# A new order for the first look-ups, transposes and grams, and a second ScalarE pass that writes the rounded tables to PSUM

## What is computed

```
e = stack([tbl_f[ids[:, f]] for f in range(27)], axis=1)      # 2048 x 27 x 128
z = e @ e^T of each sample, the entries below the diagonal    # 2048 x 351
h = concat([z, dense_ctx], axis=1)                            # 2048 x 367
h = relu(h @ W_top1 + b_top1); h = relu(h @ W_top2 + b_top2)  # 512, then 256 wide
y = h @ W_top3
```

## Time and profile before

| | |
|---|---|
| Median of 3 runs | 360.65 us (360.56 to 360.74) |
| Profiled execution, its own time | 360.54 us |
| Its span, first to last instruction | 358.7 us |
| PE busy with matmuls | 333.7 us, 93% |
| POOL busy | 250.4 us, 70% |
| DVE busy | 246.3 us, 69% |
| ACT busy | 144.4 us, 40% |

### The profile page before, as it was taken

One profiled execution on the slowest core, in us unless ns is written; L12 is line 12 of the kernel. 1 busy time (PEld: TensorE's weight loads), 2 busy tenths in 40 slices (PEclk: granted clock), 3 DMA queues, 4 the chain that ended last, 5 costly groups with the idle time before them and its releaser, 6 DMA issues.

```text
span 358.7 us, 13616 instructions
## 1 busy us (share of the span) xinstructions
PE 333.7 (93%) x6094; PEld 303.4 (85%) x6094; DVE 246.3 (69%) x329; ACT 144.4 (40%) x265; POOL 250.4 (70%) x271
## 2 busy tenths in 40 slices
PE   1879699989999989999999999999999999999896
PEld 0779499978999979898889989999899989997775
DVE  3959979975488935878197965968387955961142
ACT  2536524444433433335343453435343353435320
POOL 5777777777777777777777777777777777777200
PEclk9969989999999999999999999999999999999999
DMA  6997744534333353443333452434533443322100
GB/s 184 306 318 196 205 136 107 102 93 91 83 93 82 90 99 75 96 96 80 93 88 82 115 85 77 105 84 81 102 89 83 99 98 74 84 55 55 27 3 1
DMA packets 26155, 36.86 MB, mean 103 GB/s; under 512 B 8451, under 2 KB 20099, under 8 KB 26098
## 3 DMA queue, kind: packets, MB, share of 16 engines
q0 software_dynamic: 8448, 17.32, 20.5%
q1 hardware_dynamic: 17506, 18.16, 20.1%
q10 hardware_dynamic: 144, 0.52, 0.4%
HBM read 35.97 MB, written 0.01 MB: 100 GB/s over the span
## 4 chain that ended last, share of the span: by engine, by line
PE 57%; POOL 26%; issue 10%; DVE 3%; DMA 3%; ACT 1%; DVEq 0%; ACTq 0%
POOL rows L450 26%; PE e_banks L482 25%; PE w_banks L543 9%; PE g_banks L513 8%; PE w_banks L554 7%; PE e_banks L494 6%; DMA rows<-in_tbl,idx 2%; DVE one_hot L672 2%; PE w_banks L532 1%; DVE zt L686 1%; DMA idx<-in_idx 1%; ACT et L340 0%; ACT h L333 0%; ACT et L350 0%; DVE a L720 0%
## 5 line engine op out<-in xcount | busy, mean ns | idle before, releaser
L450 POOL DMA_INDIRECT rows<-in_tbl,idx x264 | 249.6, 945 | 82.9 <-issue 78.0
L672 DVE TENSOR_TENSOR one_hot<-ids_wide,row_no 128x1024 fp32r<-128x1024 int32 x160 | 186.3, 1215 | 76.5 <-PE e_banks L482 72.5
L482 PE MATMUL e_banks<-one_hot,table_hi 128*128 128x256 f32 x672 | 172.2, 294 | 3.4 <-issue 3.4
L482 PE MATMUL e_banks<-one_hot,table_lo 128*128 128x256 f32 x672 | 167.0, 287 | 0.0
L482 PEld LDWEIGHTS e_banks<-one_hot,table_hi 128*128 128x128 f32 x672 | 131.4, 196 | 4.4 <-issue 4.2
L482 PEld LDWEIGHTS e_banks<-one_hot,table_lo 128*128 128x128 f32 x672 | 131.6, 196 | 0.2
L350 ACT ACTIVATE et<-e_banks 128x256 f32<-128x256 f32 x84 | 57.9, 689 | 89.3 <-PE e_banks L482 89.3
L340 ACT ACTIVATE et<-e_banks 128x512 f32<-128x512 f32 (+1 forms) x68 | 45.0, 664 | 52.3 <-PE e_banks L494 51.5
L513 PEld LDWEIGHTS g_banks<-et 128*26 128x26 f32 x4096 | 41.7, 103 | 17.7 <-issue 13.3
L513 PE MATMUL g_banks<-et 128*26 128x26 f32 x4096 | 50.0, 191 | 1.8 <-DVE zt L686 1.3
L494 PE MATMUL e_banks<-ident,rows 128*128 128x128 f32 x264 | 43.0, 285 | 5.5 <-DMA rows<-in_tbl,idx 5.5
(11 more groups left out here) (25 smaller groups left out, 67.7 us busy)
## 6 DMA issues: line engine op xcount, KB each, us to landing
ids_wide<-in_ids SPq DMA_DIRECT2D x80, 128.0 KB
et<-in_kept_tables SPq DMA_DIRECT2D x10, 512.0 KB, 10.1
rows<-in_tbl,idx POOLq DMA_INDIRECT x264
et<-in_kept_tables ACTq DMA_DIRECT2D x1, 512.0 KB, 3.9
a1T<-in_ids SPq DMA_DIRECT2D x4, 128.0 KB, 10.8
w<-in_w SPq DMA_DIRECT2D x2, 256.0 KB
w<-in_W_top SPq DMA_DIRECT2D x1, 512.0 KB
w<-in_w SPq DMA_DIRECT2D x1, 222.0 KB
```

Source lines behind the costliest of these rows:

```text
L450: pool.indirect_dma_start(rows[:, k % RING, a, :], None, tables[f], bass.IndirectOffsetOnAxis(ap=idx[:, t, f:f + 1], axis=0)).then_inc(row ...
L482: last = nc.tensor.matmul(e_bank[n % E_BANKS][:, 0:UNIT], part[:, q, c, :], one_hot[:, hot_slot(o, piece), c % PIECE, :], start=(c == 0 an ...
L672: nc.vector.tensor_tensor(one_hot[:, hot_slot(o, piece), :, :], ids_place(o).unsqueeze(1).broadcast_to([P, PIECE, UNIT]), row_no[:, piece ...
```

## The change

1. **The order of the start.** Two look-ups stand ahead of the first transposes as before; the next six come at (n - 1) * 2 // 3 for look-up n, one or two behind each transposed chunk, in place of 1 + (n - 2) * 7 // 10. The eight gram pieces of tile 0 are laid over two ticks from tick 5 in place of four ticks from tick 6. The look-ups of unit 1 are spread anew by the same planner; from `("T", 2, 0)` on the list is the same as before.
2. **The rounded tables.** The steps `("HI", n)` and `ident_r` are gone. Right behind each rounding, ACT copies `table_hi` to the PSUM banks itself, one instruction of 1024 columns. Table 10, the last, now goes to `w_banks` like table 9, and ACT waits there for the rest of table 9. The zeroing of `g_banks` is gone; the first grams wait for `lo_ready` 9 in its place, that is, for the last rest that reads `g_banks`.
3. **POOL's lead.** Chunk k now waits for chunk k - ahead, with ahead = min(7, 3 + k // 4): chunks 3 to 6 wait too, and up to chunk 15 the lead is shorter.

```diff
 RING = 7
+LEAD_AT_FIRST = 3
...
-    FIRST = [("HI", n) for n in range(AHEAD)]
+    FIRST = []
     for n, q in enumerate(looked_up(0)):
-        at = 1 + (n - AHEAD) * 7 // 10
-        step = [("OH", 0, q)] + [("HI", n + AHEAD)]
-        if n == FIRST_LOOK_UPS - 1:
-            step += [("HI", m) for m in range(n + AHEAD + 1, NOH)]
         if n < AHEAD:
-            FIRST += step
+            FIRST.append(("OH", 0, q))
         else:
-            look_ups[at].append(step)
+            look_ups[(n - 1) * 2 // 3].append([("OH", 0, q)])
     for t in range(LAST_TILE):
-        at = TILE_AT[t + 1] + (t == 0)
+        at = TILE_AT[t + 1]
+        ticks = 2 if t == 0 else 4
...
-            grams[at + p * 4 // G_PIECES].append(step)
+            grams[at + p * ticks // G_PIECES].append(step)
...
-        hi_banks = [g_banks, w_banks]
+        hi_banks = [w_banks if n == NOH - 1 else (g_banks, w_banks)[n % 2] for n in range(NOH)]
+        LAST_IN_G = max(n for n in range(NOH) if hi_banks[n] is g_banks)
...
-                if k >= RING:
-                    pool.wait_ge(t_filled, k - RING + 1)
+                ahead = min(RING, LEAD_AT_FIRST + k // 4)
+                if k >= ahead:
+                    pool.wait_ge(t_filled, k - ahead + 1)
...
                 if t == 0 and p == 0:
-                    pe.wait_ge(g_banks_zeroed, 1)
+                    pe.wait_ge(lo_ready, LAST_IN_G + 1)
...
-            def rounded_table(n):
-                pe.wait_ge(hi_ready, n + 1)
...
-                    last = nc.tensor.matmul(hi_banks[n % 2][:, i, :], ident_r[:], upper[:, i * BANK:(i + 1) * BANK],
-                                            start=True, stop=True)
-                last.then_inc(hi_copied, 1)
...
             def keep_upper(n):
                 act.wait_ge(table_in[n], 16)
                 nc.scalar.activation(table_hi[:, TABLE_ORDER[n], :, :], stage(n), ACT.Copy).then_inc(hi_ready, 1)
+                act.wait_ge(hi_ready, n + 1)
+                if n == NOH - 1:
+                    act.wait_ge(lo_ready, n)
+                elif n >= 2:
+                    act.wait_ge(lo_ready, n - 1)
+                nc.scalar.activation(hi_banks[n][:, :, :].rearrange("p k d -> p (k d)"),
+                                     table_hi[:, TABLE_ORDER[n], :, :].rearrange("p c d -> p (c d)").bitcast(F32),
+                                     ACT.Copy).then_inc(hi_copied, 1)
```

More of the change, by code:

```diff
@@ L235, in dlrm_tower @@
         ident = sb("ident", [P, P])
-        ident_r = sb("ident_r", [P, P], F32R)
         row_no_i = sb("row_no_i", [P, OC], I32)
@@ L293, in dlrm_tower @@
         ids_aside_in = {o: sem(f"ids_aside_in{o}") for o in range(IDS_RING, FIRST_LOOK_UPS)}
-        g_banks_zeroed = sem("g_banks_zeroed")
         table_in = [sem(f"table_in{q}") for q in range(NOH)]
@@ L297, in dlrm_tower @@
         hi_copied = sem("hi_copied")
-        ident_r_ready = sem("ident_r_ready")
         lo_ready = sem("lo_ready")
@@ L556, in layer2 @@
                 last.then_inc(w_filled, 1)
-            def rounded_table(n):
-                pe.wait_ge(hi_ready, n + 1)
[L560 to L564, removed]
-                    last = nc.tensor.matmul(hi_banks[n % 2][:, i, :], ident_r[:], upper[:, i * BANK:(i + 1) * BANK],
-                                            start=True, stop=True)
-                last.then_inc(hi_copied, 1)
             pe.wait_ge(ident_ready, 1)
-            pe.wait_ge(ident_r_ready, 1)
             for s in STEPS:
-                if s[0] == "HI":
-                    rounded_table(s[1])
                 if s[0] == "T":
@@ L656, in keep_rest @@
                                         stage(n).rearrange("p c d -> p (c d)"),
-                                        hi_banks[n % 2][:, :, :].rearrange("p k d -> p (k d)"),
+                                        hi_banks[n][:, :, :].rearrange("p k d -> p (k d)"),
                                         ALU.subtract).then_inc(lo_ready, 1)
-                if n == NOH - 1:
-                    dve.wait_ge(lo_ready, NOH)
-                    nc.vector.memset(g_banks[:], 0.0).then_inc(g_banks_zeroed, 1)
             def make_one_hot(o):
@@ L728, in _ @@
             nc.vector.tensor_copy(row_no[:], row_no_i[:]).then_inc(row_no_ready, 1)
-            dve.wait_ge(ident_ready, 1)
-            nc.vector.tensor_copy(ident_r[:], ident[:]).then_inc(ident_r_ready, 1)
             dve.wait_ge(row_no_ready, 1)
```

## The result

The changed kernel takes **363.46 us** in the median (360.44 to 364.37, 19 runs), the kernel before 360.21 us in the same comparison (359.51 to 361.94, 19 runs): ratio **1.0063**, 95% interval 1.0048 to 1.0079. The prediction said 360.6. The times fall into two groups: nine runs at 360.4 to 362.6 and ten at 363.4 to 364.4. No run of the kernel before lies in the upper group, and the profiled execution (363.64 us, span 361.8) does.

A forecast was written before the change was run, and what follows sets the result against it. POOL's gather pace was taken as the bound before chunk 24, PE and POOL nearly together behind it. POOL 0, start 0, from chunk 14 on 0 left 360.5 us; the median 0.1 above gave 360.6, range 360.1 to 361.5.

The forecast's parts named there:

- The list is the same from chunk 10 on, so the rest is the same.: From chunk 10 on: PE, some 5 us ahead, waits for POOL's rows, reaches chunk 14 as before, and nothing later changes.
- from chunk 14 on 0: Term of the sum for everything from chunk 14 to the end: no change, 0 us.
- my rivals: The clock falls (0.14 briefly, 0.07 longer), POOL held (0.04), ACT late (0.03), chunk 24's landing in time (0.10).
- The lead holds nothing: POOL's gathers at the start: the shorter lead delays none, 1.9 us to spare at chunk 0's transposes; term 0.
- PE's early lead turns into waiting: Chunks 10 to 14: PE's 5 us of lead becomes waiting for POOL's rows, gaining nothing.
- ScalarE's pass, taken as 1.06: ACT's table copy at the start: 1.06 us each, between 0.56 and 1.9.
- The start: Start of the program: chunk 7 transposed at 47.0 instead of 51.66, chunk 10 at about 60 instead of 64.89; term 0.
- Chunk 14: PE's wait for rows at chunk 14: 2 to 3 us, ending at 79.53 as before.
- that rival: After chunk 14's longer wait PE's clock falls: briefly 361.0 us, chance 0.14; at length or twice 362.5, chance 0.07.
- The landing of chunk 24: Rival: if chunk 24's rows land in time, PE runs 1.1 us earlier to the last chunk: 360.2 us, chance 0.10.
- two bounds within 0.7 to 1.0 us of each other: Behind chunk 24, PE's work and POOL's gathers bound the kernel almost equally; an earlier PE could get 0.4 us.

The follow-up runs named there:

- f3: Kernel before with only ScalarE's second pass in place of the table products, old order and lead, TensorE's stream 53 instructions shorter: 364.00 us, ratio 1.0102.
- f4: Kernel before with 203 instructions of already met waits added on TensorE, spread over the transposes: 374.25 us, ratio 1.0370.
- e12: Kernel before with only POOL's new, shorter lead of the gathers: 360.42 us, ratio 0.9990.
- g1: Kernel before with only the new order of look-ups, transposes and grams, stream length unchanged: 360.65 us, ratio 0.9998.
- f1: The changed kernel itself, run again without edits: 361.43 us, ratio 1.0048 to the kernel before.
- f2: Changed kernel with 53 instructions (106 already met waits) put back at TensorE's start: 361.60 us, ratio 1.0033 to the kernel before.
- e11: Kernel before with only ScalarE's second pass, plus 53 instructions of met waits given back to TensorE: 361.60 us, ratio 1.0017.
- e4: Kernel before with only ScalarE's second pass, old order and lead, TensorE's stream 53 instructions shorter: ratio 1.0058.
- e6, e2: Kernel before with 203 instructions of already met waits on TensorE, ahead of transposes and at the start: ratio 1.0275.
- e9: The changed kernel itself, run again as base for its padded forms: ratio 1.0086 to the kernel before.

## Why the prediction was wrong

**The step that failed** is "The list is the same from chunk 10 on, so the rest is the same." The list of work is; the position of its instructions in the stream is not. What was said to be free is the removal of 53 instructions 300 us earlier, and with them went the cover of a block's load. In the prediction's sum this is the term "from chunk 14 on 0": it was 3.1 us of the span, of which 0.44 had come about by the last transposes and 2.5 are the stands. They are shown for the profiled run. That they lift half of the runs by 2 to 3 us rests on the counts and on f3 and f4. None of my rivals had it, and the page had the queue in its section 3. A piece of 0.31 us of plain issue stood in the last stretch of the kernel before, where there is no other work. I had no reason for it and did not ask.

**Right.** The lead holds nothing (e12, and no piece over 0.30 us in POOL's line). PE's early lead turns into waiting; the order alone is worth nothing (g1, within 0.2%). ScalarE's pass, taken as 1.06:

```profile
L586 ACT ACTIVATE w_banks<-table_hi x6: 1027/1028/1030, 10.2 to 42.6; 128x1024 f32<-128x1024 f32 x6
L586 ACT ACTIVATE g_banks<-table_hi x5: 1027/1028/1029, 6.5 to 34.7; 128x1024 f32<-128x1024 f32 x5
```

**Mis-sized.** *The start.* Chunk 7 at 47.0 came at 50.87, chunk 10 at 60 came at 63.62. The rows are DVE's, ACT's and PE's timelines:

```profile
28.29 1.22 DVE L664 TENSOR_TENSOR one_hot<-a1T,row_no 128x1024 fp32r<-128x1024 int32 x1 [1.87 <-PE e_banks L481]
```

```profile
42.55 1.03 ACT L586 ACTIVATE w_banks<-table_hi 128x1024 f32<-128x1024 f32 x1 [2.53 <-DVE table_lo L650]
43.51 0.66 ACT L348 ACTIVATE et<-e_banks 128x256 f32<-128x256 f32 x1
```

```profile
44.23 2.09 PE L513 MATMUL g_banks<-et 128*26 128x26 f32 x128 [5.42 <-ACT et L348]
```

DVE did not run through. It was held 1.87 + 0.42 us by look-ups behind the transposes of chunk 2, which waited 2.72 for their rows; I had looked at the waits for chunks 0 and 1 only. So the last rest started at 43.61 and not at 41.2, ACT's drain ended at 44.17 and not 41.9, and the grams started at 44.23. They then took 2.09 + 1.80 us, not two times 1.3; the granted clock between 44.23 and 50.87 was 0.78.
*Chunk 14.* I expected a wait of 2 to 3 us that ends at 79.53; it was 1.07, and ended at 78.75, since the landing came sooner and the lead was smaller. The waits of 1.07 and below did not make the clock fall, which that rival needed: it was 1.00 from 78.8 to 83.6.
*The landing of chunk 24.* The rival said that PE would run on if it came in time. It did: no wait at 130.96. PE kept its 0.7 to 0.9 us until chunk 50, where POOL's rows stopped it. So "two bounds within 0.7 to 1.0 us of each other" held, but the meeting place is not fixed. It moves with the landings of single gathers.
*POOL's start.* 0.4 us later with idx, 0.5 in f1 and f2, 0.3 in e11, 0.1 in f3, and not at all in g1 and e12. It comes with ScalarE's pass; how, I have not tested.

**Open.** Why the same program loads its block at 340.02 in one run and at 338.73 in another. With one traced run of the changed kernel in each group, that is as far as the difference between the groups can be followed. In the first, PE has 11956 instructions behind it as the load begins, in the second 11753. Both have passed the border before, at 11713: the first load begins 2.5 us behind that, the second 0.9. In e4, e6 and f4, which stood 2.2 us and more, it is 2.5 to 3.1. So the long stands are late loads. In f1, f3, e9 and e2, whose borders lie at the same places against PE's wait for `zt`, it is 0.9 to 1.1. What makes the load late in one run and not in another is not known. The trace shows when a packet starts, not what asked for it. Open too are the 1.4 and 0.9 us by which the medians of f2 and e11 lie above the kernel before.

No version beat the kernel before. The shorter lead alone (e12, 0.9990) and the new order alone (g1, 0.9998) have intervals that hold 1.

## What to carry to other kernels

An edit that removes instructions moves every later border of 256 instructions in that engine's stream. Where an engine runs on short instructions with no idle time, list its plain "issue" pieces, compare them with the instruction queue's packets, and ask which wait now covers each load. A stall in the last stretch had nothing to hide it here, so look there first. When a comparison gives two groups of times, count the groups and don't only compare medians. And idle instructions that are meant as a neutral filler have a price: here 0.19 us for six waits on an engine without idle time, and 256 of them at the start held POOL for 2.85 us.

## What the runs showed of the hardware

- TensorE's instructions arrive in packets of 16,384 bytes, 48 in this program. A block's work started 1.23 us after it had landed at the soonest (945 borders in 20 traces), and 1.24 to 1.59 us where PE had stood for it. A stand at a border took from 0.2 to 2.75 us. PE stops 63 instructions short of a multiple of 256 in the records.
- Gram matmuls of 26 columns use up a block faster than it arrives. The piece that follows the last wait in the kernel before is 128 matmuls with their weight loads, a block of 256 instructions, in 1.26 us; the load of a block takes 0.9 to 1.3 us in the rows above, and 1.3 to 1.6 us pass behind it:

```profile
338.76 1.26 PE L513 MATMUL g_banks<-et 128*26 128x26 f32 x128 [1.31 <-DVE zt L686]
```

- The clock need not fall after such a stand: 8 matmuls behind one of 2.21 us took 1.92 us (the kernel after, granted clock 1.00). Behind one of 2.22 us they took 3.71 us (e4, clock 0.50), behind one of 2.49 us 3.41 us (f4, 0.55).
